# A code-book feed-forward loop with the bias as contracted rows, GELUs over two PSUM banks, and the far gates on GpSimd

## The chip, the cores and the metric

The kernel runs as one program on one core of a Trainium2 chip. It computes a whole tower of four layers. The metric is the device time of one execution in microseconds (us); the number quoted is the median of three runs. The core's engines have instruction streams of their own: TensorE (PE in the rows, PEld for its weight loads), VectorE (DVE), ScalarE (ACT), GpSimd (POOL) and SyncE (SP), which here starts transfers. They meet only at semaphores: an instruction waits until a counter has reached a value, and adds to a counter when it is done.

## The reference

The change lies in one stage, the feed-forward part of layer 2, which looks up small networks in code books. For each of 2048 tokens and each of S = 8 sub-spaces, with D = 192, R = 16, M = 64 codes, K = 4 chosen, H = 32 hidden units and G = 64:

```python
z = jnp.einsum('nd,sdr->nsr', xf, P)
scores = jnp.einsum('nsr,smr->nsm', z, C)
topv, topi = jax.lax.top_k(scores, K)
w = jax.nn.softmax(topv, axis=-1)
W1g = W1[sidx, topi]; b1g = b1[sidx, topi]
W2g = W2[sidx, topi]; b2g = b2[sidx, topi]
h = jax.nn.gelu(jnp.einsum('nsr,nskrh->nskh', z, W1g) + b1g)
yl = jnp.einsum('nskh,nskhr->nskr', h, W2g) + b2g
comb = jnp.einsum('nskr,nsk->nsr', yl, w).reshape(N, S * R)
out = jax.nn.gelu(comb @ G1 + g1b) @ G2 + g2b
```

Here xf is the layer-normalised residual, and out is added to the residual. Each code m of sub-space s has its own small network with W1[s, m] (16 by 32), b1, W2 (32 by 16) and b2; a token uses the four codes with the best scores, weighted by w.

## The kernel before

The kernel does not gather. It evaluates all 64 codes of every sub-space for every token and multiplies the hidden values by a gate, which is w for a chosen code and zero for the others. `codes_stage` (L1549) does it in `NG = 4` groups of `GT = 512` tokens. A group takes `STEPS = 32` steps: 16 for sub-spaces 0 to 3, then 16 for sub-spaces 4 to 7 (a half each). A step handles `QS = 4` units, one for each of the four sub-spaces, and a unit holds four codes of 32 hidden units, thus 128 rows by 512 tokens.

In a step, for unit j:

- TensorE forms the up product (L1740), one PSUM bank `up` each, four banks. The weights are `w1r` and the tokens `zr`, both bf16 with 96 contracted rows: a float is split into three bf16 parts, and six products of parts stand below one another in the rows.
- ScalarE applies GELU with the bias b1 as a column (L1879) and writes into `hp`, one of `HOLD = 3` step buffers in SBUF.
- VectorE multiplies by the gate (L2021). The near gates (j = 0, 1) are spread to 128 rows by a product of TensorE into the PSUM tile `gate` (L1747). The far gates (j = 2, 3) come with a DMA of 512 KB a step, issued by SyncE, from a scratch in DRAM into `wide_gates`, a ring of `GRING = 5` step slots (`bring_gates`).
- TensorE adds the down products of the step (L1767, float32: two rows of the trace for each of the four) to the accumulator `comb`. In the program's order they stand after the units of the next step, one step behind.

At a half's end ScalarE copies `comb` to `comb_t` (`keep_comb`, L1871), and TensorE starts the next half with bias products for b2 (L1758, L1762). The tail of a group (`first_last` L1724, ScalarE's GELU, `second_last` L1731, VectorE's `add_out` L2027 to the residual) runs in steps 2 to 4 of the next group.

The preparation of the next group is interleaved with the steps, as the loops over k write it out: projection (L1676), scores (L1682), the eight best of each row and the marking of four (L1967, L1981), exponentials (L1857, between two activation-table loads), the spreading of z to 96 rows (L1690), the gates' normalisation, splitting and transposition (L1698, L1708). All of TensorE's pieces go through one PSUM bank, `misc`, that ScalarE empties (`keep`, L1830). The last group prepares nothing. Ahead of the loop the same steps run for group 0, and w1 is split on VectorE and spread to `w1r` by TensorE.

The order on each engine is the order in which the program is written; no scheduler moves anything. The semaphores that matter are `up_ready`, `h_ready` (a GELU is done), `gate_ready`, `gated` (a multiplication is done), `downed` (the down products of a step), `comb_kept`, and `gates_in` (a transfer landed).

Of the kernel before, what the change touches and what calls it, by code (L numbers as in the profile page):

```python
# [1497 lines left out]
KR = SR * len(PAIRS)  # L1498
QS = SS // 2
# [4 lines left out]
BANKS = 4  # L1504
GBANKS = 2
HOLD = 3
# [3 lines left out]
GRING = 5  # L1510
# [49 lines left out]
def codes_stage(nc, m, a):  # L1560
    with Stage(nc, "cod") as s:
# [3 lines left out]
        sel_w = s.sb("sel_w", [P, 4, NPART, KR], BF16)  # L1565
        sel_g = s.sb("sel_g", [P, NBLK, P], BF16)
        b1 = s.sb("b1", [P, SS * HT])
# [6 lines left out]
        w1r = s.sb("w1r", [KR, SS, SM * SH], BF16)  # L1574
        zr = [s.sb(f"zr{i}", [KR, SS, GT], BF16) for i in range(2)]
# [3 lines left out]
        hp = [s.sb(f"hp{i}", [P, QS, GT]) for i in range(HOLD)]  # L1579
        ex = s.sb("ex", [P, GS * SS, SM])  # L1580
# [18 lines left out]
        first_bank = up + gate + [misc]  # L1599
        names = ("w_in p_in w1_in w1_split first_ready first_kept zeroed misc_ready misc_kept z_high z_low z_rest_ready z_mid "  # L1600
                 "shifted exped weighted w_high w_rest w_mid w_low up_ready gate_ready h_ready gated downed "
                 "comb_kept b2_ready dve act_own").split()
        (w_in, p_in, w1_in, w1_split, first_ready, first_kept, zeroed, misc_ready, misc_kept, z_high, z_low, z_rest_ready, z_mid,
         shifted, exped, weighted, w_high, w_rest, w_mid, w_low, up_ready, gate_ready, h_ready, gated, downed,
         comb_kept, b2_ready, dve, act_own) = (s.sem(n) for n in names)
        gates_out = s.sem("gates_out")
        gates_in = [s.sem(f"gates_in{i}") for i in range(GRING)]
        N_IN = 10
# [13 lines left out]
        def _(sp):  # L1622
# [3 lines left out]
            for dst, src in ((sel_w[:].bitcast(I16), "sel_w"), (sel_z[:].bitcast(I16), "sel_z"),  # L1626
                             (sel_g[:].bitcast(I16), "sel_g"), (b2, "S_b2"), (b2d[:], "S_b2d"), (b1[:], "S_b1"), (w2[:], "S_w2"),
                             (g1[:], "S_g1"), (g1b[:], "S_g1b"), (g2[:], "S_g2")):
                sp.dma_start(dst, a[src]).then_inc(w_in, 16)

# [28 lines left out]
        def _(pool):  # L1659
            nc.gpsimd.memset(wp[:], 0.0).then_inc(zeroed, 1)  # L1660
            pool.wait_ge(zeroed, 1)
            nc.gpsimd.memset(last_h[SG:SG + 1, :], 1.0).then_inc(zeroed, 1)

        @block.tensor
        def _(pe):
# [69 lines left out]
            def unit(g, k, j):  # L1735
                u = g * UNITS + k * QS + j
                sub, f = QS * (k // HT) + j, code_of(k, j)
                if u >= BANKS:
                    pe.wait_ge(h_ready, u - BANKS + 1)
                nc.tensor.matmul(up[u % BANKS][:], w1r[:, sub, f * P:(f + 1) * P], zr[g % 2][:, sub, :],  # L1740
                                 start=True, stop=True).then_inc(up_ready, 1)
                if j >= QP:
                    return
                if u >= QS:
                    pe.wait_ge(gated, u - QS + 1)
# [1837 lines left out]
```

## Time and profile before

| what | value |
|---|---|
| median of three runs | 3345.11 us (3338.17 to 3347.05) |
| profiled execution | 3335.59 us |
| its span | 3333.8 us |
| mean granted TensorE clock | 0.85 of full speed |
| TensorE busy | 2390.9 us (72%) |
| VectorE busy | 2309.3 us (69%) |
| ScalarE busy | 1595.2 us (48%) |
| GpSimd busy | 940.1 us (28%) |
| code-book loop, 2158 to 2621 us | 463 us |

Busy times are sums over the whole tower, whose stages have different limits, so they say little on the stage in question. The last line is a stretch of the timeline; its four groups take 124, 126, 125 and 88 us. In the tables a clock of 1.00 stands for 2.4 GHz, 0.50 for 1.2 GHz.

### The profile page before, as it was taken

What the parts mean: (1) busy time and instruction counts of PE and PEld (TensorE: products, weight loads), DVE (VectorE), ACT (ScalarE), POOL (GpSimd) and SP (SyncE); (2) the same over time, 40 slices, a digit from 0 to 9 for tenths busy, and PEclk for the clock granted to TensorE, in tenths of its full rate; (3) what the DMA queues carried; (4) which work ended last, traced back from release to release, by engine and by line L of the source; (5) the groups of instructions that cost most, each with busy time, mean ns of one, the idle gap of its engine ahead of it and who ended that gap; (6) DMA issues with size and microseconds to landing.
All of it is one profiled execution on the core that took longest, in us unless ns stands there. A gap on an engine that the chain in (4) does not pass through costs nothing. (4 is left out here: it accounts for less than half of the span.)

```text
span 3333.8 us, 38681 instructions
## 1 busy us (share of the span) xinstructions
PE 2390.9 (72%) x12580; PEld 1437.0 (43%) x12620; DVE 2309.3 (69%) x5830; ACT 1595.2 (48%) x2954; POOL 940.1 (28%) x466
## 2 busy tenths in 40 slices
PE   5869985889898877699931112688889788774457
PEld 4646652334343334499721111323222366663335
DVE  5753333999999996211278998588888699998521
ACT  3221114667665642111116773677878546654211
POOL 2000003777676761367300000000000033344032
PEclk9969996899999987799965555799999899997578
DMA  1230001111111100511100000234435400000221
GB/s 54 38 115 1 1 15 69 51 51 51 51 51 51 51 0 0 177 39 41 56 12 1 1 0 2 101 122 151 152 114 189 144 1 1 1 1 1 120 85 56
DMA packets 81796, 185.27 MB, mean 56 GB/s; under 512 B 35197, under 2 KB 52827, under 8 KB 76251
## 3 DMA queue, kind: packets, MB, share of 16 engines
q1 hardware_dynamic: 75452, 170.56, 15.3%
q0 software_dynamic: 6144, 12.25, 1.2%
q8 instruction: 101, 1.65, 0.2%
q14 instruction: 99, 0.81, 0.1%
HBM read 165.91 MB, written 24.77 MB: 57 GB/s over the span
## 5 line engine op out<-in xcount | busy, mean ns | idle before, releaser
L2243 POOL TENSOR_TENSOR mam_st<-mam_du,mam_b_rows 128x1536 f32<-128x1536 f32 x128 | 439.6, 3441 | 172.9 <-PE mam_ysum L2312 172.4
L2473 DVE TENSOR_TENSOR_SCAN mam_st<-mam_da,mam_st 128x512 f32<-128x512 f32 x384 | 441.1, 1204 | 35.9 <-ACT mam_da L2413 18.2
L2312 PE MATMUL mam_ysum<-mam_st,held_ident 128*128 128x512 f32 x768 | 389.7, 648 | 2.2 <-DVE mam_st L2479 2.2
L1879 ACT ACTIVATE cod_hp<-cod_up,cod_b 128x512 f32<-128x512 f32 x512 | 317.0, 704 | 84.3 <-PE cod_up L1740 84.3
L2413 ACT ACTIVATE mam_da<-mam_delta,mamw_decay 128x508 f32<-128x508 f32 x384 | 254.2, 683 | 185.9 <-DVE mam_st L2473 151.0
L2595 POOL TENSOR_TENSOR att_probs<-att_se,att_neg 128x1536 f32<-128x1536 f32 x16 | 55.0, 3441 | 811.8 <-DVE att_neg L2805 811.8
L2479 DVE TENSOR_TENSOR mam_st<-mam_st,mam_c_ps 128x1536 f32<-128x1536 f32 x128 | 224.4, 1753 | 17.0 <-PE mam_c_ps L2307 13.5
L2312 PEld LDWEIGHTS mam_ysum<-mam_st,held_ident 128*128 128x128 f32 x768 | 159.4, 208 | 167.5 <-issue 160.3
L692 DVE SCALAR_TENSOR_TENSOR held_h<-x_dn,held_gate,held_h 128x192 f32<-128x192 f32 x256 | 89.1, 410 | 182.5 <-PE x_dn L659 180.8
L2805 DVE MATCH_REPLACE8 att_neg<-att_top,att_neg 128x128 f32<-128x128 f32 x768 | 201.2, 275 | 0.3
L2021 DVE TENSOR_TENSOR cod_hp<-cod_hp,cod_gate 128x512 f32<-128x512 f32 x256 | 163.3, 678 | 47.4 <-ACT cod_hp L1879 46.9
L1740 PE MATMUL cod_up<-cod_zr,cod_w1r 96*128 96x512 bf16 x512 | 181.0, 392 | 15.2 <-ACT cod_hp L1879 9.4
L2021 DVE TENSOR_TENSOR cod_hp<-cod_hp,cod_wide_gates 128x512 f32<-128x512 f32 x256 | 164.6, 683 | 25.0 <-ACT cod_hp L1879 24.9
L2798 DVE MAX8 att_top<-att_neg 128x8 f32<-128x128 f32 x768 | 154.7, 278 | 21.3 <-ACT att_neg L2721 14.2
L1767 PE MATMUL cod_comb<-cod_hp,cod_w 128*16 128x512 f32 x1024 | 140.1, 620 | 26.3 <-DVE cod_hp L2021 25.6
L682 ACT ACTIVATE x_ht<-x_up 128x512 f32<-128x512 f32 x96 | 52.1, 595 | 211.5 <-PE x_up L649 211.5
L456 POOL TENSOR_TENSOR held_h<-held_h,n_y 128x768 f32<-128x768 f32 x4 | 7.4, 1846 | 484.2 <-DVE n_y L492 484.0
L659 PEld LDWEIGHTS x_dn<-x1w_w,x_ht 128*128 128x128 f32 x768 | 123.5, 190 | 35.6 <-issue 35.6
L925 ACT ACTIVATE gr_ht<-gr_up 128x512 f32<-128x512 f32 x80 | 39.2, 491 | 205.9 <-PE gr_up L863 205.9
L659 PE MATMUL x_dn<-x1w_w,x_ht 128*128 128x192 f32 x768 | 137.4, 332 | 0.0
L993 DVE TENSOR_TENSOR gr_o<-gr_dn,gr_w2c 128x192 f32<-128x192 f32 x40 | 14.3, 358 | 173.0 <-PE gr_dn L874 173.0
L2307 PE MATMUL mam_c_ps<-mam_c_part,mamw_pick 96*128 96x512 bf16 x128 | 52.2, 408 | 106.8 <-DVE mam_st L2479 101.9
(551 smaller groups left out, 5338.1 us busy)
## 6 DMA issues: line engine op xcount, KB each, us to landing
cod_wide_gates<-gate_scratch SPq DMA_DIRECT2D x128, 512.0 KB, 3.9
mam_b_rows<-b_scratch SPq DMA_DIRECT2D x32, 1024.0 KB, 7.3
slot_scratch<-in_slot_fresh SPq DMA_DIRECT2D x2, 3860.0 KB, 14.5
sw_w<-in_L_w SPq DMA_DIRECT2D x1, 6144.0 KB, 18.5
gr_w<-in_L_w SPq DMA_DIRECT2D x1, 5376.0 KB, 41.7
gr_w<-in_L_w SPq DMA_DIRECT2D x1, 4608.0 KB
sw_w<-in_L_w SPq DMA_DIRECT2D x1, 4608.0 KB, 31.0
gr_rows<-slot_scratch SPq DMA_DIRECT2D x40, 96.5 KB, 2.0
```

The costliest lines, as they stand in the source:

```text
L659: last = nc.tensor.matmul(dn[x % 2][:, t, 0:D], ht[(g * NT + f) % NHT][:, t * P:(t + 1) * P], w2_sb[:, f, :], start=(f == first[e]), stop= ...
L1740: nc.tensor.matmul(up[u % BANKS][:], w1r[:, sub, f * P:(f + 1) * P], zr[g % 2][:, sub, :], start=True, stop=True).then_inc(up_ready, 1)
L1767: last = nc.tensor.matmul(comb[32 * j:32 * j + SR, :], w2[:, sub * HT + code_of(k, j), :], hp[step % HOLD][:, j, :], start=False, stop=(k ...
L1879: nc.scalar.activation(hp[step % HOLD][:, j, :], up[u % BANKS][:], ACT.Gelu_apprx_tanh, bias=b1[:, sub * HT + f:sub * HT + f + 1]).then_in ...
L2021: nc.vector.tensor_tensor(at, at, by, ALU.mult).then_inc(gated, 1)
L2243: nc.gpsimd.tensor_tensor(st[it % N_ST][:], du[r % 2][:], along(b_rows[:, p % RING, n % PIECE, :], 1, [P, MC, MT]), ALU.mult)\
L2312: last = nc.tensor.matmul(ysum[:, c, :], m.ident[:], st[it % N_ST][:, c, :], start=False, stop=(it % DS == DS - 1))
L2413: nc.scalar.activation(live(da[:, c, :], r % 2), live(delta[r % 2][:, c, :], r % 2), ACT.Exp, scale=decay[:, c, n:n + 1]).then_inc(exp_rea ...
L2473: nc.vector.tensor_tensor_scan(fs, fa, fs, 0.0, ALU.mult, ALU.add).then_inc(scanned, 1)
L2479: nc.vector.tensor_tensor(x[:], x[:], along(c_ps[:], 1, [P, MC, MT]), ALU.mult).then_inc(weighted, 1)
L2798: last = nc.vector.max(top[:, n, :], cut[:, n, :])
L2805: last = nc.vector.match_replace(rev, top[:, n, :], rev, -BIG)
```

## The change

Six things change in the stage.

1. The bias b1 becomes three more contracted rows (99 in place of 96): the rows 96 to 98 of `w1r` hold b1's three bf16 parts, those of `zr` hold ones. VectorE splits b1 at the stage's start; SyncE carries the parts through a new scratch in DRAM into `w1r`. GpSimd sets the ones.
2. `up` becomes two tiles of two banks. `pair(g, k, h)` forms two units, and one GELU of 128 x 1024 without a bias takes both.
3. `gate` becomes one tile of two banks, and VectorE multiplies both near units in one operation.
4. Both far units are multiplied on GpSimd, in one operation of 128 x 1024, announced on a new counter `pool_gated`; down products and SyncE's transfers wait for it as well.
5. There are four step buffers, and the down products of step s - 2 (`LAG = 2`) are issued in step s, after the first pair, ahead of the gates and of the second pair. The transfer ring for far gates has four slots.
6. The preparation, the tail and the copy of `comb` move with it, the first two by two steps, the copy by one.

The diff, cut to its core (line numbers are left out; the shifts of the preparation on ScalarE and VectorE are like the one shown on TensorE):

```diff
@@ sizes @@
+KB = KR + NPART
-BANKS = 4
-GBANKS = 2
-HOLD = 3
+HOLD = 4
+LAG = 2
-GRING = 5
+GRING = 4
+N_GATED = 1
@@ tiles @@
-        w1r = s.sb("w1r", [KR, SS, SM * SH], BF16)
-        zr = [s.sb(f"zr{i}", [KR, SS, GT], BF16) for i in range(2)]
+        w1r = s.sb("w1r", [KB, SS, SM * SH], BF16)
+        zr = [s.sb(f"zr{i}", [KB, SS, GT], BF16) for i in range(2)]
-        up = [s.psum(f"up{i}", [P, 512]) for i in range(BANKS)]
-        gate = [s.psum(f"gate{i}", [P, 512]) for i in range(GBANKS)]
+        up = [s.psum(f"up{i}", [P, 2, 512]) for i in range(2)]
+        gate = s.psum("gate", [P, QP, 512])
@@ SyncE @@
+            sp.dma_start(b1[:], a["S_b1"]).then_inc(b1_in, 16)
...
+            sp.wait_ge(b1_split, NPART)
+            for p in range(NPART):
+                sp.dma_start(m.b1_scratch[p], b1_part[p][:]).then_inc(b1_out, 16)
+            sp.wait_ge(b1_out, 16 * NPART)
+            sp.dma_start(w1r[KR:KB].rearrange("o s c -> o (s c)"),
+                         m.b1_scratch.rearrange("n r p -> n (r p)")).then_inc(b1_rows, 16)
...
-                    sp.wait_ge(gated, QS * (step - GRING + 1))
+                    sp.wait_ge(gated, N_GATED * (step - GRING + 1))
+                    sp.wait_ge(pool_gated, step - GRING + 1)
@@ GpSimd @@
+            for i in range(2):
+                nc.gpsimd.memset(zr[i][KR:KB, :, :], 1.0).then_inc(ones_set, 1)
+
+            for step in range(NG * STEPS):
+                pool.wait_ge(h_ready, 2 * step + 2)
+                pool.wait_ge(gates_in[step % GRING], 16 * (step // GRING + 1))
+                at = hp[step % HOLD][:, QP:, :]
+                nc.gpsimd.tensor_tensor(at, at, wide_gates[:, step % GRING], ALU.mult).then_inc(pool_gated, 1)
@@ TensorE @@
+            def pair(g, k, h):
+                step = g * STEPS + k
+                if step:
+                    pe.wait_ge(h_ready, 2 * step + h - 1)
+                for i in range(2):
+                    j = 2 * h + i
+                    sub, f = QS * (k // HT) + j, code_of(k, j)
+                    last = nc.tensor.matmul(up[h][:, i, :], w1r[:, sub, f * P:(f + 1) * P], zr[g % 2][:, sub, :],
+                                            start=True, stop=True)
+                last.then_inc(up_ready, 1)
+
+            def gates(g, k):
+                step = g * STEPS + k
+                if step:
+                    pe.wait_ge(gated, N_GATED * (step - 1) + 1)
+                for j in range(QP):
+                    ...
+                last.then_inc(gate_ready, 1)
@@ down @@
-                pe.wait_ge(gated, QS * (step + 1))
+                pe.wait_ge(gated, N_GATED * (step + 1))
+                pe.wait_ge(pool_gated, step + 1)
@@ TensorE's loop; the pieces of the preparation and of the tail two steps later @@
-                        if k == 2:
+                        if k == 4:
                             first_last(g - 1)
...
-                    for j in range(QS):
-                        unit(g, k, j)
-                    if g + k:
-                        down(g * STEPS + k - 1)
+                    pair(g, k, 0)
+                    if g * STEPS + k >= LAG:
+                        down(g * STEPS + k - LAG)
+                    gates(g, k)
+                    pair(g, k, 1)
@@ ScalarE @@
+            def pair(g, k, h):
+                step = g * STEPS + k
+                act.wait_ge(up_ready, 2 * step + h + 1)
                 if step >= HOLD:
                     act.wait_ge(downed, step - HOLD + 1)
-                nc.scalar.activation(hp[step % HOLD][:, j, :], up[u % BANKS][:], ACT.Gelu_apprx_tanh,
-                                     bias=b1[:, sub * HT + f:sub * HT + f + 1]).then_inc(h_ready, 1)
+                nc.scalar.activation(hp[step % HOLD][:, 2 * h:2 * h + 2, :], up[h][:], ACT.Gelu_apprx_tanh)\
+                    .then_inc(h_ready, 1)
...
-                    if g + k > 1 and k % HT == 1:
+                    if g + k > LAG and k % HT == LAG:
                         keep_comb((g * STEPS + k) // HT - 1)
@@ VectorE @@
+            def near_gates(g, k):
+                step = g * STEPS + k
+                v.wait_ge(h_ready, 2 * step + 1)
+                v.wait_ge(gate_ready, step + 1)
+                at = hp[step % HOLD][:, 0:QP, :]
+                nc.vector.tensor_tensor(at, at, gate[:], ALU.mult).then_inc(gated, 1)
...
+            v.wait_ge(b1_in, 16)
+            nc.vector.tensor_copy(b1_part[0][:], b1[:]).then_inc(b1_split, 1)
+            ...
             v.wait_ge(w1_in, 16)
...
-                    for j in range(2):
-                        unit(g, k, j)
+                    near_gates(g, k)
```

On TensorE, near the end of the last group before the change (`cod_comb` products are down products, `cod_up` up products, `cod_gate` the spread near gates):

```order
L1767 MATMUL cod_comb<-cod_hp,cod_w 16x512 x4
L1740 MATMUL cod_up<-cod_zr,cod_w1r 128x512
L1747 MATMUL cod_gate<-cod_wt,cod_sel_g 128x512
L1740 MATMUL cod_up<-cod_zr,cod_w1r 128x512
L1747 MATMUL cod_gate<-cod_wt,cod_sel_g 128x512
L1740 MATMUL cod_up<-cod_zr,cod_w1r 128x512 x2
L1767 MATMUL cod_comb<-cod_hp,cod_w 16x512 x4
```

The same place after it, at the very end of the loop:

```order
L1764 MATMUL cod_up<-cod_zr,cod_w1r 128x512 x4
L1797 MATMUL cod_comb<-cod_hp,cod_w 16x512 x4
L1775 MATMUL cod_gate<-cod_wt,cod_sel_g 128x512 x2
L1764 MATMUL cod_up<-cod_zr,cod_w1r 128x512 x2
L1797 MATMUL cod_comb<-cod_hp,cod_w 16x512 x8
```

The down products moved from behind all four up products of a step to between the first pair and the gates, and are now those of the step two back; a row of four up products is the second pair of one step and the first pair of the next. At the end two steps of down products are left over.

On ScalarE, around the exponentials in the first group before the change (`cod_zr` and `cod_comb_t` are copies out of PSUM, `cod_hp` the GELUs):

```order
L1879 ACTIVATE cod_hp<-cod_up,cod_b 128x512 x4
L1830 ACTIVATE cod_zr<-cod_misc 96x512
L1857 ACT_TABLE_LOAD
L1857 ACTIVATE cod_ex<-cod_ex 128x2048
L1879 ACT_TABLE_LOAD
L1879 ACTIVATE cod_hp<-cod_up,cod_b 128x512 x4
L1830 ACTIVATE cod_zr<-cod_misc 96x512
L1879 ACTIVATE cod_hp<-cod_up,cod_b 128x512 x4
L1871 ACTIVATE cod_comb_t<-cod_comb 128x512
```

And after it:

```order
L1912 ACTIVATE cod_hp<-cod_up 128x1024 x2
L1864 ACTIVATE cod_zr<-cod_misc 96x512
L1891 ACT_TABLE_LOAD
L1891 ACTIVATE cod_ex<-cod_ex 128x2048
L1912 ACT_TABLE_LOAD
L1912 ACTIVATE cod_hp<-cod_up 128x1024 x2
L1905 ACTIVATE cod_comb_t<-cod_comb 128x512
L1864 ACTIVATE cod_zr<-cod_misc 96x512
```

The exponentials kept their distance from the other pieces, while the copy of `comb` at the half boundary came one step nearer to them: two GELUs stand between, where eight did.

## Rows read from the trace of the kernel before

**Rows 1.** Windows of the four groups: start:end, length, busy of PE, PEld, DVE, ACT, POOL, PEclk.
```profile
2158.00:2282.00 124.00, 106.82 (x555) 33.11 (x566) 103.63 (x258) 99.57 (x166) 0.00 (x0) 0.93 0.46 154
2282.00:2408.00 126.00, 107.89 (x576) 34.46 (x588) 105.91 (x262) 99.44 (x166) 0.00 (x0) 0.96 0.42 141
2408.00:2533.00 125.00, 108.86 (x573) 34.47 (x580) 105.12 (x261) 98.58 (x164) 0.00 (x0) 0.95 0.43 139
2533.00:2621.00 88.00, 83.95 (x486) 23.01 (x486) 78.11 (x130) 77.22 (x130) 0.00 (x0) 1.00 0.51 170
```

**Rows 2.** TensorE's timeline, two steps without preparation: start, duration, operation.
```profile
2402.91 1.05 PE L1767 MATMUL cod_comb<-cod_hp,cod_w 128*16 128x512 f32 x8
...
2403.89 0.39 PE L1740 MATMUL cod_up<-cod_zr,cod_w1r 96*128 96x512 bf16 x1
...
2405.31 1.05 PE L1767 MATMUL cod_comb<-cod_hp,cod_w 128*16 128x512 f32 x8
```

**Rows 3.** Groups of instructions by shape, whole run: busy, mean ns, idle before.
```profile
L2243 POOL TENSOR_TENSOR mam_st<-mam_du,mam_b_rows 128x1536 f32<-128x1536 f32 x128 | 439.6, 3441 | 172.9 <-PE mam_ysum L2312 172.4
...
L1879 ACT ACTIVATE cod_hp<-cod_up,cod_b 128x512 f32<-128x512 f32 x512 | 317.0, 704 | 84.3 <-PE cod_up L1740 84.3
...
L2021 DVE TENSOR_TENSOR cod_hp<-cod_hp,cod_gate 128x512 f32<-128x512 f32 x256 | 163.3, 678 | 47.4 <-ACT cod_hp L1879 46.9
...
L1767 PE MATMUL cod_comb<-cod_hp,cod_w 128*16 128x512 f32 x1024 | 140.1, 620 | 26.3 <-DVE cod_hp L2021 25.6
...
L682 ACT ACTIVATE x_ht<-x_up 128x512 f32<-128x512 f32 x96 | 52.1, 595 | 211.5 <-PE x_up L649 211.5
...
L456 POOL TENSOR_TENSOR held_h<-held_h,n_y 128x768 f32<-128x768 f32 x4 | 7.4, 1846 | 484.2 <-DVE n_y L492 484.0 <-ACT n_y L538 0.2
...
L1849 ACT ACTIVATE cod_z_part<-held_xw 128x1024 bf16<-128x1024 f32 x4 | 4.2, 1057 | 0.0
```

**Rows 4.** ScalarE's and TensorE's timelines at a half boundary.
```profile
2410.28 0.60 ACT L1871 ACTIVATE cod_comb_t<-cod_comb 128x512 f32<-128x512 f32 x1
...
2410.93 1.47 PE L1758 MATMUL cod_comb<-cod_wt,cod_b_part 128*32 128x512 bf16 x12 [0.76 <-ACT cod_comb_t L1871]
...
2413.31 1.05 PE L1767 MATMUL cod_comb<-cod_hp,cod_w 128*16 128x512 f32 x8
```

**Rows 5.** TensorE's timeline, pieces of the preparation.
```profile
2304.71 1.98 PE L1676 MATMUL cod_misc<-held_xt,cod_proj 96*128 96x512 f32 x4
...
2306.53 0.38 PE L1740 MATMUL cod_up<-cod_zr,cod_w1r 96*128 96x512 bf16 x1
...
2308.91 1.13 PE L1682 MATMUL cod_misc<-cod_codes,held_xw 128*128 128x256 f32 x4
...
2338.51 0.85 PE L1690 MATMUL cod_misc<-cod_z_part,cod_sel_z 128*96 128x512 bf16 x3
```

**Rows 6.** TensorE's timeline, the second product of a group's tail.
```profile
2422.24 0.92 PE L1731 MATMUL cod_misc<-cod_g,cod_last_h 65*128 65x192 f32 x4 [0.49 <-DVE held_h L2027]
```

**Rows 7.** ScalarE's timeline around the exponentials.
```profile
2343.84 0.59 ACT L1830 ACTIVATE cod_zr<-cod_misc 96x512 bf16<-96x512 f32 x1
...
2348.96 2.42 ACT L1879 ACTIVATE cod_hp<-cod_up,cod_b 128x512 f32<-128x512 f32 x4
```

**Rows 8.** TensorE's timeline, down products after a wait.
```profile
2328.60 1.91 PE L1767 MATMUL cod_comb<-cod_hp,cod_w 128*16 128x512 f32 x8 [1.39 <-DVE cod_hp L2021]
...
2334.45 1.06 PE L1767 MATMUL cod_comb<-cod_hp,cod_w 128*16 128x512 f32 x8
```

**Rows 9.** TensorE's timeline, the stage's first down product.
```profile
2167.74 1.05 PE L1767 MATMUL cod_comb<-cod_hp,cod_w 128*16 128x512 f32 x8
```

**Rows 10.** DMA issues: KB each, median us from issue to landing.
```profile
cod_wide_gates<-gate_scratch SPq DMA_DIRECT2D x128, 512.0 KB, 3.9
```

**Rows 11.** GpSimd's and VectorE's timelines in the Mamba stage.
```profile
602.02 3.43 POOL L2243 TENSOR_TENSOR mam_st<-mam_du,mam_b_rows 128x1536 f32<-128x1536 f32 x1 [2.82 <-PE mam_ysum L2312]
...
601.90 3.45 DVE L2473 TENSOR_TENSOR_SCAN mam_st<-mam_da,mam_st 128x512 f32<-128x512 f32 x3 [0.68 <-ACT mam_da L2413]
```

More of the change, by code:

```diff
@@ L1579, in codes_stage @@
         hp = [s.sb(f"hp{i}", [P, QS, GT]) for i in range(HOLD)]
+        at_first = hp[NPART][:].rearrange("p j t -> p (j t)")
+        sel_cols = 4 * NPART * KR // 2
+        sel_w = at_first[:, 0:sel_cols].bitcast(BF16).rearrange("p (q n r) -> p q n r", q=4, n=NPART)
+        b1 = at_first[0:SS * HT, sel_cols:sel_cols + P]
+        b1_part = [at_first[0:SS * HT, sel_cols + P + i * P // 2:sel_cols + P + (i + 1) * P // 2].bitcast(BF16)
+                   for i in range(NPART)]
         ex = s.sb("ex", [P, GS * SS, SM])
@@ L1733, in second_last @@
                 last.then_inc(misc_ready, 1)
[L1735 to L1745, printed above, removed]
-                half, code = f // NBLK, f % NBLK
-                nc.tensor.matmul(gate[j][:], sel_g[:, code, :], wt[g % 2][:, 2 * (QP * (k // HT) + j) + half, :],
-                                 start=True, stop=True).then_inc(gate_ready, 1)
+            def pair(g, k, h):
[13 more added lines that the diff above has]
+                for j in range(QP):
+                    f = code_of(k, j)
+                    half, code = f // NBLK, f % NBLK
+                    last = nc.tensor.matmul(gate[:, j, :], sel_g[:, code, :],
+                                            wt[g % 2][:, 2 * (QP * (k // HT) + j) + half, :], start=True, stop=True)
+                last.then_inc(gate_ready, 1)
             def down(step):
@@ L1812, in _ @@
[L1812 to L1818 removed]
+                        if 7 <= k < 9:
+                            misc_turn(turn + Z_AT + k - 7)
+                            project(g + 1, k - 7, misc, misc_ready)
@@ new lines, in _ @@
+                        if 9 <= k < 13:
+                            misc_turn(turn + SC_AT + k - 9)
+                            score(g + 1, k - 9, misc, misc_ready)
+                        if 14 <= k < 22:
+                            misc_turn(turn + ZR_AT + k - 14)
+                            spread_z(g + 1, k - 14, misc, misc_ready)
+                        if 25 <= k < 27:
+                            misc_turn(turn + GF_AT + k - 25)
+                            turn_gates(g + 1, k - 25, misc, misc_ready)
@@ L1819, in _ @@
+                        if 27 <= k < 31:
+                            misc_turn(turn + WT_AT + k - 27)
+                            turn_w(g + 1, k - 27, misc, misc_ready)
+                    pair(g, k, 0)
[3 more added lines that the diff above has]
+                    pair(g, k, 1)
                 if g + 1 < NG:
                     pe.wait_ge(misc_kept, prep_turn(g + 1) + N_PREP)
-            down(NG * STEPS - 1)
+            for i in range(LAG):
+                down(NG * STEPS - LAG + i)
@@ L2080, in _ @@
[L2080 to L2092 removed]
+                        if 10 <= k < 14:
+                            v.wait_ge(misc_kept, prep_turn(g + 1) + SC_AT + k - 10 + 1)
+                            bests(k - 10)
@@ new lines, in _ @@
+                        if 15 <= k < 19:
+                            mark_best(k - 15, 0)
+                        if 19 <= k < 23:
+                            weights(g + 1, k - 19)
+                        if 20 <= k < 24:
+                            normed(k - 20)
+                        if 24 <= k < 28:
+                            low_w(g + 1, k - 24)
+                    if g + 1 < NG:
+                        if k == 11:
+                            low_z(g + 1)
+                        if 11 <= k < 15:
+                            shift(g + 1, k - 11)
+                        if 15 <= k < 19:
+                            mark_best(k - 15, 1)
+                        if 19 <= k < 23:
+                            totals(k - 19)
+                        if 22 <= k < 26:
+                            rest_w(g + 1, k - 22)
```

133 lines of the change are left out of this document (42 added, 91 removed).

## The prediction

> **What bounds the kernel now.** I read the granted clock and the 40 slices first, to find the stage; then busy times in four windows, one for each group of 512 tokens; then TensorE's timeline inside a group; then the durations of the operations; then what ended each wait.
>
> The code loop takes 463 us of the span of 3333.8, about 14%; nothing else in the kernel changes [rows 1]. The last group, which prepares no successor, takes 88 us, and there TensorE is busy 84 and granted the full 2.4 GHz; the two middle groups take 126 and 125 [rows 1]. So there are two limits. In a step without preparation TensorE sets the pace: down products start at 2402.91 and again at 2405.31, a step of 2.40 us; it splits into 0.98 (2402.91 to 2403.89) for the four down products and 1.42 for six bf16 products, 0.22 each and a switch of 0.1 [rows 2]. In a step with preparation VectorE does: 27.8 us more in a middle group than in the last (105.91 less 78.11) come on top of four multiplications a step of 678 ns [rows 1, 3], and 25.6 of TensorE's idle time in the loop stands before the down products, released by the multiplication [rows 3]. The step is a chain, up product, GELU, multiplication, down product, one step deep, so each late multiplication stops TensorE.
>
> **The change part by part.** The hand-over from one engine to the next costs 0.05 us (ScalarE's copy ends at 2410.28 + 0.60 = 2410.88, TensorE starts at 2410.93) [rows 4].
>
> VectorE loses the two far multiplications, and its two near ones become one operation of 1024 columns, at most 2 x 678 = 1.36 us [rows 3]: 43.5 a group, and with 27.8 of preparation 71 of some 119. It is then no bound, and its waits before the down products go.
>
> ScalarE: four GELUs of 704 ns become two over two banks without bias. The GELU without bias takes 595 at 512 columns, so 1.19 for two; a copy over 1024 takes 1057 [rows 3]. I take 1.06, between 0.70 and 1.19, since the copy has the same width. That is 67.8 a group, against 77 in the last one now [rows 1].
>
> GpSimd has no operation in the loop now [rows 1], and gets 128 multiplications of 1024 columns from two tiles in SBUF. Its multiplications take 3441 at 1536 columns and its additions 1846 at 768 [rows 3]: a slope of 2.077 ns a column, so 1846 + 256 x 2.077 = 2378 ns, 2.38 us, bounded by 1.85 and 3.44. By itself that fits under the step, but it is in the chain.
>
> The chain now: counted from the start of down(s-2), the down products end at 0.98; the two gates at 1.42; the first of pair 1 starts there, the second at 1.64 and lasts 0.39; GELU 1 starts at 2.08 and ends at 3.14; GpSimd runs from 3.19 to 5.57; down(s) may start at 5.62. These are two steps, so 2.81 a step, above TensorE's own 2.40. The cause is the place of the down products ahead of pair 1: its up products wait behind the products two steps back, which wait for GpSimd. With 1.85 or 3.44 for GpSimd a step is 2.54 or 3.34. A fourth step buffer doesn't loosen it, for it is TensorE's order that closes the loop. VectorE's near gates start at 1.47 and end by 2.83, so 2.8 us of preparation may come between before they delay anything.
>
> Steps with preparation are set by TensorE once the sum of 2.40 and the piece exceeds 2.81. The projection costs 1.82 (2304.71 to 2306.53), with a switch 1.92; a score 1.13 less the overlap of 0.16 seen there, with a switch 1.07; a spread 0.85 less 0.16, 0.68 [rows 5]. The tail's first product I set like a projection, the second at 0.9 from its 0.92 [rows 6]; the transposes at 0.8, an estimate from the spread.
>
> A middle group, step by step. Step 2: the comb tile must be copied before the next bias products. GELU 1 of the step before starts 2.08 after down, then comes GELU 0, then the copy, which ends at about 4.6; the bias products take 2.38 (2410.93 to 2413.31) [rows 4]: 7.0. Steps 4 to 12: 9 x 2.40 = 21.6, pieces 1.92 + 2 x 0.9 + 2 x 1.92 + 4 x 1.07 = 11.8, and 3.8 of waits: twice 1.5, since the next product needs the addition to the residual, which now stands behind a multiplication whose gates come late in the step (0.05 + 1.36 + 0.5 for three quarters of 678 ns, less 0.44 for pair 1), and 0.8, since the first score's copy stands behind a GELU and the rounding of z: 37.2. Seven spread steps at 3.08: 21.6. Step 18: ScalarE's two table loads and exponentials keep it from GELU for 5.1 us (2343.84 to 2348.96) [rows 7]; then come GELU 1, GELU 0 and the comb copy, which ends at 8.7, and 2.38: 11.1. After such a wait TensorE ran at 1.2 GHz once: down to down took 5.85 (2328.60 to 2334.45), against 2.40 + 0.68 for such a step, so 2.8 lost [rows 8]; I take 1.7, between 0 and 2.8: 12.8. Six steps with transposes: 6 x 3.2 = 19.2. The other eight, two of them behind a stall at 2.40: 21.7. Sum 119.5, against 125.5 now.
>
> The first group: 10.7 to its first down product, 2167.74 now and one step later afterwards, though a shorter one: 2168.7 [rows 9]; then 119.5 less 7.0 (step 2), 6.7 (the tail's 3.7 and its two waits of 1.5), 5.4 (steps 0 and 1), plus 1.9 for what is left of step 2: 102.3. Together 113, now 124. The last group: two boundaries 14.0, three tail steps 7.2 + 3.7 + 1.5 = 12.4, 26 steps at 2.76 (2.81 but for the three behind a stall) 71.8, the last step 0.4 and its drain 5.62 + 1.05 = 6.7: 105, now 88. So the last group loses 17 and the first three win 23.
>
> Sum: 113 + 119.5 + 119.5 + 105 = 457 against 463: -6. The setup gains four VectorE operations on 128 columns and two more trips through DRAM. These lie beside TensorE's products that spread w1, but the small operations stand ahead of the splitting of w1: +1.3, between 0 and 2.7 (a transfer of 512 KB lands in 3.9 [rows 10], a small one sooner, if w1's own doesn't hide it). In all -5. The ones rows cost nothing: GpSimd sets them while the weights are being spread. Ring of 4 for the far gates: SP may issue a transfer once GpSimd has finished the step four earlier, three steps or 8.4 us ahead of use, and it lands in 3.9 [rows 10]; behind SP's wait stand only later transfers. The down product's added wait holds up the gates and pair 1, which is the loop above. 99 rows in place of 96 I take to cost TensorE nothing: the gates' products have 128, and all six together take 1.42 [rows 2].
>
> **From the trace to the time.** The profiled execution took 3335.6, its span 3333.8. The median of the runs is 3345.1, so the profiled one is 9.5 below it. 3335.6 - 5 = 3331, and for the median 3345.1 - 5 = 3340.
>
> **The rivals.** First, that the chain does not bind: if GpSimd needs 1.56 or less (5.62 - 2 x 0.41 = 4.80, two steps of 2.40), or TensorE issues pair 1 earlier than I think, then the last group returns to about 91, and in the other groups eight steps win 0.4 each: 14 + 3 x 3.3, less what the boundaries keep, some -18 more: 3322. For it speaks that spans on GpSimd are rough; against it that 768 and 1536 columns give 2.40 and 2.24 ns a column, nowhere near 1.5. Chance 0.15.
>
> Second, the clock, on the slower side. Each of the seven half boundaries now keeps TensorE idle for about 2.2 us in one piece (the copy behind two GELUs). Before, 0.76 there left it at full speed [rows 4], while two waits of 1.39 close together brought 1.2 GHz [rows 8]. If each boundary loses the 2.8 us of that spell: 7 x 2.8 = 20, and 3360. It decides from the point where an idle piece of 2.2 us is enough by itself. Chance 0.2.
>
> Third, GpSimd and VectorE hinder each other. In the Mamba stage VectorE's scans, with two inputs in SBUF, start at 601.90 and run three in 3.45 while GpSimd's multiplication runs from 602.02 for 3.43, and neither is stretched [rows 11]: so here the trace shows no exclusion. Were there one, up to 27.8 of preparation a group [rows 1] would hold GpSimd up, and GpSimd's 2.38 VectorE in turn; about half of the preparation has two tile inputs, so between 14 and 28 a group, I take 20: 3340 + 60 = 3400. Chance 0.08.
>
> The Trainium skill, "SBUF — State Buffer", section "SBUF: two separate sides", says that a VectorE operation with two SBUF inputs and a GpSimd operation that reads SBUF share a port pair, held for a whole instruction, so that one blocks the other. By that rule the third rival would be the forecast; [rows 11] disagree with it, and so it gets little.
>
> That the change does not do what it says is covered by none of these; for that and mishaps elsewhere (code loading, transfers) 0.05.
>
> **How the numbers follow.** The forecast's case has 0.52, with a range of its own from 3329 (GpSimd at 2.2, no slow spell) to 3352 (GpSimd at 2.6, 2.8 at every step 18). About 0.3%, 10 us, is what a measurement of this kernel can tell from no change. Faster than 3335: a third of the forecast's case and nearly all of the first rival, with 0.02 of the rest: 0.34. Slower than 3355: most of the second, the third, and 0.03: 0.28. Within: 0.38. The range takes in the first rival with a margin for GpSimd at 1.85, and the second with some of GpSimd at 2.6 and more: 3314 to 3366; the third lies outside.
>
> **What would show it.** A plain step of 2.81 in the last group, which then takes 105, TensorE waiting before the comb product for GpSimd; GpSimd's multiplication at 2.38; GELU at 1.06 and VectorE no longer the one that releases the down products; about 119 in the middle groups; a wait of some 5 us at step 18. Wrong it would be if the last group stays near 90 (no loop), if the granted clock falls at the half boundaries (second rival), or if GpSimd's operation is longer in the groups with preparation than in the last (third).

## The result and the profile after

The changed kernel takes 3381.64 us (median of four, 3377.31 to 3386.27) against 3341.64 for the kernel before in its four runs: a ratio of 1.0123, 95% interval 1.0104 to 1.0142. It is slower by 40 us, where 5 us less was forecast, and lies above the range.

The stage accounts for it. From the first projection to the first down product it took 70.3 us before (2097.47 to 2167.74) and 73.9 after (2106.94 to 2180.82); from the first down product to the last, 452.4 before and 491.0 after: 3.6 + 38.6 = 42. The profiled execution is 51 longer than that of before because it already stands 9.5 later when the stage begins, in code that did not change; in most of the runs below the stage begins at 2094 to 2100 again, so this is the spread of single executions.

The four groups of the changed kernel, for [rows 1], with the same columns:

```profile
2170.00:2300.00 130.00, 109.08 (x564) 33.67 (x565) 76.78 (x162) 86.93 (x101) 76.79 (x32) 0.88 0.44 142
2300.00:2434.00 134.00, 112.07 (x586) 35.12 (x584) 78.34 (x165) 85.65 (x101) 78.66 (x33) 0.91 0.41 131
2434.00:2568.00 134.00, 111.52 (x587) 34.75 (x588) 77.97 (x165) 86.54 (x102) 78.24 (x33) 0.91 0.41 132
2568.00:2674.00 106.00, 88.00 (x493) 23.54 (x486) 38.79 (x33) 62.60 (x67) 75.47 (x32) 0.97 0.42 144
```

The last group takes 106, as forecast (105). The groups with preparation take 130 and 134, where 113 and 119.5 were forecast: the whole error is there. VectorE's busy time fell by only 27 in a middle group (105.1 to 78.0), though it lost more work than that: its multiplications fell from 78.1 to 38.8 in the last group. The other 12 are operations that became longer. The groups of instructions in the loop, for [rows 3], show which:

```profile
L2047 DVE TENSOR_TENSOR cod_hp<-cod_hp,cod_gate 128x1024 f32<-128x1024 f32 x128 | 155.7, 1217 | 229.9 <-PE cod_gate L1775 204.5 <-ACT cod_hp L1912 25.2 <-issue 0.2
L2031 DVE TENSOR_TENSOR cod_ex<-cod_ex,cod_total 128x512 f32<-128x512 f32 x12 | 19.1, 1593 | 0.0
...
L2019 DVE SCALAR_TENSOR_TENSOR cod_ex<-held_xw,cod_ex 128x512 f32<-128x512 f32 x12 | 18.7, 1556 | 0.0
L2005 DVE TENSOR_TENSOR cod_ex<-held_xw,held_logits 128x512 f32<-128x512 f32 x12 | 18.1, 1506 | 0.3
...
L1994 DVE TENSOR_TENSOR cod_z_part<-cod_ex,cod_z_part 128x1024 bf16<-128x1024 f32 x3 | 9.4, 3118 | 0.0
L2025 DVE TENSOR_REDUCE cod_total<-cod_ex 128x8 f32<-128x512 f32 x12 | 8.1, 676 | 0.1
```

In the kernel before, the operations of L2031, L2019 and L2005 took 684, 685 and 685 ns and that of L1994 1215. All four have two inputs in SBUF. Their rows there, under the line numbers of the kernel before:

```profile
L1974 DVE TENSOR_TENSOR cod_ex<-held_xw,held_logits 128x512 f32<-128x512 f32 x12 | 8.2, 685 | 0.3
L1988 DVE SCALAR_TENSOR_TENSOR cod_ex<-held_xw,cod_ex 128x512 f32<-128x512 f32 x12 | 8.2, 685 | 0.0
L2000 DVE TENSOR_TENSOR cod_ex<-cod_ex,cod_total 128x512 f32<-128x512 f32 x12 | 8.2, 684 | 0.0
L1963 DVE TENSOR_TENSOR cod_z_part<-cod_ex,cod_z_part 128x1024 bf16<-128x1024 f32 x3 | 3.6, 1215 | 0.0
```

The reduction (one input, 677 before) and the near gates (one input in PSUM, 1217 against 1214 in far_on_vector below, where GpSimd is idle) kept their length. GpSimd's multiplication, in the same list, whose waits are for ScalarE:

```profile
L1684 POOL TENSOR_TENSOR cod_hp<-cod_hp,cod_wide_gates 128x1024 f32<-128x1024 f32 x128 | 309.2, 2415 | 247.8 <-ACT cod_hp L1912 247.2
```

VectorE's wait stands in busy time and not in idle time, so no releaser names it. One step shows how it works, the fourteenth of a middle group, VectorE first:

```profile
2348.67 3.12 DVE L1994 TENSOR_TENSOR cod_z_part<-cod_ex,cod_z_part 128x1024 bf16<-128x1024 f32 x1
2351.89 2.64 DVE L2005 TENSOR_TENSOR cod_ex<-held_xw,held_logits 128x512 f32<-128x512 f32 x1
...
2354.49 1.18 DVE L2047 TENSOR_TENSOR cod_hp<-cod_hp,cod_gate 128x1024 f32<-128x1024 f32 x1
```

GpSimd in the same stretch:

```profile
2348.34 2.36 POOL L1684 TENSOR_TENSOR cod_hp<-cod_hp,cod_wide_gates 128x1024 f32<-128x1024 f32 x1 [0.52 <-ACT cod_hp L1912]
2351.20 2.78 POOL L1684 TENSOR_TENSOR cod_hp<-cod_hp,cod_wide_gates 128x1024 f32<-128x1024 f32 x1 [0.50 <-ACT cod_hp L1912]
```

and TensorE:

```profile
2350.85 1.05 PE L1797 MATMUL cod_comb<-cod_hp,cod_w 128*16 128x512 f32 x8 [0.35 <-POOL cod_hp L1684]
2355.73 1.03 PE L1775 MATMUL cod_gate<-cod_wt,cod_sel_g 128*128 128x512 bf16 x2 [3.83 <-DVE cod_hp L2047]
```

VectorE's 3.12 ends 1.1 after GpSimd's 2.36 has ended at 2350.70, its 2.64 ends 0.55 after 2353.98: each did all but about 0.13 of its own 1.22 and 0.69 us of work after GpSimd was done. GpSimd's second multiplication, begun while VectorE's first operation still ran, is 0.4 longer, as it had to wait in turn. Who starts first is not held up: an operation with two inputs in SBUF that began before GpSimd's kept its 1.22, and GpSimd's, begun 0.9 before its end, took 3.12 in place of 2.36:

```profile
2344.37 1.22 DVE L1990 TENSOR_TENSOR cod_ex<-held_xw,cod_z_part 128x1024 f32<-128x1024 f32 x1
...
2344.69 3.12 POOL L1684 TENSOR_TENSOR cod_hp<-cod_hp,cod_wide_gates 128x1024 f32<-128x1024 f32 x1 [1.36 <-ACT cod_hp L1912]
```

So these two engines do not meet only at semaphores, as was said of all of them at the start: here each waits for the other with no semaphore between them. In step 14 the near gates stand behind both operations, and TensorE waits 3.83 us to overwrite the gate tile: 8.8 us for a step that should take 3.1.

### The profile page after: what moved, and what is told of

Same layout as the page of the kernel before. It is cut to its first block and busy times, and to the rows that moved or that the text cites. A ratio compares the mean times of both kernels' runs of the same rounds, so it can differ in the third digit from the quotient of the medians.

```text
span 3384.4 us, 37961 instructions
## 1 busy us (share of the span) xinstructions
PE 2404.2 (71%) x12620; PEld 1438.5 (43%) x12620; DVE 2191.1 (65%) x5450; ACT 1540.7 (46%) x2698; POOL 1257.2 (37%) x596
## 5 line engine op out<-in xcount | busy, mean ns | idle before, releaser
L2503 DVE TENSOR_TENSOR_SCAN mam_st<-mam_da,mam_st 128x512 f32<-128x512 f32 x384 | 441.1, 1204 | 35.9 <-ACT mam_da L2443 18.2
L1684 POOL TENSOR_TENSOR cod_hp<-cod_hp,cod_wide_gates 128x1024 f32<-128x1024 f32 x128 | 309.2, 2415 | 247.8 <-ACT cod_hp L1912 247.2
L2342 PE MATMUL mam_ysum<-mam_st,held_ident 128*128 128x512 f32 x768 | 397.4, 659 | 2.2 <-DVE mam_st L2509 2.2
L1912 ACT ACTIVATE cod_hp<-cod_up 128x1024 f32<-128x1024 f32 x256 | 254.5, 1021 | 149.8 <-PE cod_up L1764 147.3
L2047 DVE TENSOR_TENSOR cod_hp<-cod_hp,cod_gate 128x1024 f32<-128x1024 f32 x128 | 155.7, 1217 | 229.9 <-PE cod_gate L1775 204.5
L2509 DVE TENSOR_TENSOR mam_st<-mam_st,mam_c_ps 128x1536 f32<-128x1536 f32 x128 | 224.4, 1753 | 16.2 <-PE mam_c_ps L2337 12.8
L1764 PE MATMUL cod_up<-cod_zr,cod_w1r 99*128 99x512 bf16 x512 | 151.2, 396 | 2.9 <-ACT cod_hp L1912 1.6
```

What stands on the lines that cost most here:

```text
L1684: nc.gpsimd.tensor_tensor(at, at, wide_gates[:, step % GRING], ALU.mult).then_inc(pool_gated, 1)
L1764: last = nc.tensor.matmul(up[h][:, i, :], w1r[:, sub, f * P:(f + 1) * P], zr[g % 2][:, sub, :], start=True, stop=True)
L1912: nc.scalar.activation(hp[step % HOLD][:, 2 * h:2 * h + 2, :], up[h][:], ACT.Gelu_apprx_tanh)\
L2047: nc.vector.tensor_tensor(at, at, gate[:], ALU.mult).then_inc(gated, 1)
L2342: last = nc.tensor.matmul(ysum[:, c, :], m.ident[:], st[it % N_ST][:, c, :], start=False, stop=(it % DS == DS - 1))
L2503: nc.vector.tensor_tensor_scan(fs, fa, fs, 0.0, ALU.mult, ALU.add).then_inc(scanned, 1)
```

## The experiments

The table gives the time between a group's first down product and the next group's (the last group: to its last one), read from the down products' rows of each run, and the ratio to the kernel before in the runs that were taken together with each (their medians lie between 3337 and 3342).

| kernel | g0 | g1 | g2 | g3 | median us | ratio (95%) |
|---|---|---|---|---|---|---|
| before | 120.1 | 125.4 | 125.1 | 81.7 | 3341.6 | |
| changed | 129.0 | 133.2 | 133.1 | 95.8 | 3381.6 | 1.0123 (1.0104 to 1.0142) |
| one_input | 113.7 | 120.2 | 119.8 | 94.2 | 3340.5 | 1.0012 (0.9996 to 1.0028) |
| pair1_first | 120.2 | 126.2 | 126.2 | 82.5 | 3347.3 | 1.0039 (1.0022 to 1.0055) |
| copy_back | 120.9 | 126.5 | 124.9 | 92.1 | 3354.5 | 1.0058 (1.0037 to 1.0079) |
| far_on_vector | 121.9 | 126.1 | 126.2 | 83.1 | 3348.9 | 1.0038 (1.0018 to 1.0058) |
| all_vector | 120.1 | 125.6 | 124.3 | 81.7 | 3341.3 | 1.0014 (1.0001 to 1.0026) |
| all_gpsimd | 122.4 | 126.4 | 126.3 | 82.5 | 3347.8 | 1.0033 (1.0023 to 1.0043) |
| far_copy | 111.7 | 118.3 | 120.9 | 81.0 | 3327.0 | 0.9961 (0.9947 to 0.9974) |
| far_copy_add | 112.9 | 115.0 | 116.4 | 79.4 | 3312.6 | 0.9918 (0.9905 to 0.9932) |
| gpsimd_copy_add | 120.6 | 122.6 | 122.8 | 90.6 | 3341.3 | 1.0007 (0.9981 to 1.0032) |

**The two-input operations taken away.** Each of the seven preparation operations, for groups 1 to 3, becomes a reduction, as here:

```diff
+                if g:
+                    nc.vector.tensor_reduce(lone[:, t, 16:24], ex[:, cols, :], AX.X, ALU.add).then_inc(weighted, 1)
+                    return
                 nc.vector.tensor_tensor(ex[:, cols, :], ex[:, cols, :], along(total[:, cols], 2, full),
                                         ALU.mult).then_inc(weighted, 1)
```

> Seven preparation operations of VectorE in the loop (for groups 1 to 3), those with two inputs in SBUF, are replaced by reductions that read one of the two inputs, so they take as long but their results are missing (the gates of groups 1 to 3 are not the reference's). Theory A, exclusion: VectorE's two-input operations and GpSimd's multiplication wait for each other whole. Then those seven go back from 1.5 to 3.1 us to 0.4 to 1.2 us, the step with the first spread from 8.8 to about 3.1, the steps with the gates' sums from 4.3, 5.7 and 6.6 to about 2.8 each, a middle group from 133 to about 119, the last group stays at 95.8, and the time falls by about 40 us, to 3340. Theory B, VectorE's work is simply late behind the near gates: the replaced operations are as long as the unstretched ones, the waits stay, a middle group stays within 130 to 133 and the time within 10 us of 3381.

Theory A to the number: a middle group 120, the time 3340.5. The reductions do not stretch, and GpSimd is down to its own length:

```profile
L1685 POOL TENSOR_TENSOR cod_hp<-cod_hp,cod_wide_gates 128x1024 f32<-128x1024 f32 x128 | 302.4, 2363 | 211.3 <-ACT cod_hp L1913 210.8
...
L2045 DVE TENSOR_REDUCE cod_lone<-cod_ex 128x8 f32<-128x512 f32 x12 | 8.1, 678 | 0.0
```

VectorE had as many operations as in the changed kernel, each about as long as the original when nothing meets it, so late work was not the cause; their two SBUF inputs were. That a reduction also writes less does not explain it: the near gates write 1024 columns and kept 1.22 us beside GpSimd. Not all of the 13 is the operations themselves: the half boundary between two groups fell from 8.5 to 6.9, as its bias products ran at 2.4 GHz, while steps 6 and 7 became longer by about as much.

**The second pair first.**

```diff
                     pair(g, k, 0)
-                    if g * STEPS + k >= LAG:
-                        down(g * STEPS + k - LAG)
                     gates(g, k)
                     pair(g, k, 1)
+                    if g * STEPS + k >= LAG:
+                        down(g * STEPS + k - LAG)
```

> On TensorE the gates and the second pair are issued ahead of the down products of the step two back; nothing else changes. Theory A, the chain through GpSimd closes only because the second pair stands behind the down products: a plain step of the last group falls from 2.84 to about 2.42 (GpSimd's 2.37 and a hand-over), the last group from 95.8 to about 84, and the middle groups by 5 or less, as their waits are others: 3381 less 12 less 15 at most, 3355 to 3369. Theory B, the pace is GpSimd's latency wherever the products stand: the plain step stays at 2.84 and the time at 3381.

The chain closes where theory A put it: the plain step of the last group is 2.39 and 2.54 in turn, 2.47 on average, and the group falls by 13. TensorE's rows of two such steps:

```profile
2597.43 1.05 PE L1797 MATMUL cod_comb<-cod_hp,cod_w 128*16 128x512 f32 x8
...
2599.82 1.05 PE L1797 MATMUL cod_comb<-cod_hp,cod_w 128*16 128x512 f32 x8
...
2602.36 1.05 PE L1797 MATMUL cod_comb<-cod_hp,cod_w 128*16 128x512 f32 x8
```

In the changed kernel these go in pairs of 5.66 (2652.46 to 2658.12), with GpSimd as the releaser of every second one:

```profile
2652.46 1.05 PE L1797 MATMUL cod_comb<-cod_hp,cod_w 128*16 128x512 f32 x8 [0.82 <-POOL cod_hp L1684]
...
2654.85 1.05 PE L1797 MATMUL cod_comb<-cod_hp,cod_w 128*16 128x512 f32 x8
...
2658.12 1.05 PE L1797 MATMUL cod_comb<-cod_hp,cod_w 128*16 128x512 f32 x8 [0.82 <-POOL cod_hp L1684]
```

It also took 7 from the middle groups, more than the 5 expected (2.9 of them at the half boundary, which fell from 8.5 to 5.6), so that 3347.3 lies below the expected 3355.

**The copy back by a step.**

```diff
-                    if g + k > LAG and k % HT == LAG:
+                    if g + k > LAG - 1 and k % HT == LAG - 1:
                         keep_comb((g * STEPS + k) // HT - 1)
```

> ScalarE's copy of the comb tile goes back by one step, between the two GELUs of step 1 (or 17) of a half, where it stood before the change; the rest is as in the changed kernel. Theory A, at a half boundary TensorE pays an idle piece of 2 us or more and, because of it, a spell at 1.2 GHz: the idle piece goes, the bias products go back from 3.8 to 2.4 us, the boundary falls from 8.4 to about 5.2, and that of step 18 from 12.5 to about 8.5: 25 us in all, 3356. Theory B, the bias products are slow for another reason: they stay at 3.8, and only the idle pieces go: about 15 us, 3366.

As theory A said: 3354.5, a boundary of 4.77 (5.2 expected). Step 18 fell further than expected, from 12.5 to 5.8, but the step after it rose from 3.0 to 4.6. The boundary in the last group of the changed kernel, TensorE:

```profile
2621.28 1.05 PE L1797 MATMUL cod_comb<-cod_hp,cod_w 128*16 128x512 f32 x8
...
2625.83 2.01 PE L1787 MATMUL cod_comb<-cod_wt,cod_b_part 128*32 128x512 bf16 x12 [2.09 <-ACT cod_comb_t L1905]
...
2629.61 1.23 PE L1797 MATMUL cod_comb<-cod_hp,cod_w 128*16 128x512 f32 x8
```

and with the copy back:

```profile
2585.72 1.05 PE L1797 MATMUL cod_comb<-cod_hp,cod_w 128*16 128x512 f32 x8
...
2588.11 1.47 PE L1787 MATMUL cod_comb<-cod_wt,cod_b_part 128*32 128x512 bf16 x12
...
2590.49 1.05 PE L1797 MATMUL cod_comb<-cod_hp,cod_w 128*16 128x512 f32 x8
```

The idle 2.09 is gone, and the bias products with it go from 3.78 to 2.38, the time that they take at 2.4 GHz (granted clock 0.61 from 2625.8 to 2629.6 in the changed kernel, 1.00 from 2588.1 to 2590.4 here). But the idle piece alone does not decide: in one_input the same 2.09 stands at the same place and the bias products take 2.38, at a granted clock of 1.00:

```profile
2577.78 1.47 PE L1788 MATMUL cod_comb<-cod_wt,cod_b_part 128*32 128x512 bf16 x12 [2.09 <-ACT cod_comb_t L1906]
2580.16 1.05 PE L1798 MATMUL cod_comb<-cod_hp,cod_w 128*16 128x512 f32 x8
```

What else brings the clock down there stays open.

**The far gates on VectorE.** GpSimd's loop goes, and between the two blocks of preparation of each step VectorE does:

```diff
+            def far_gates(g, k):
+                ...
+                nc.vector.tensor_tensor(at, at, wide_gates[:, step % GRING], ALU.mult).then_inc(pool_gated, 1)
```

> Both far gates are multiplied by VectorE in one operation of 1024 columns in place of GpSimd; all else stays as in the changed kernel, TensorE's order too. Theory A, exclusion and the chain through GpSimd's 2.4 us are what was lost: the plain step falls from 2.84 to 2.40, the last group from 95.8 to about 85, the seven two-input operations take their 0.4 to 1.2 us again, a middle group falls from 133 to about 118: some 55 us in all, 3325. Theory B, the two-step lag with its later gates and its half boundaries is what costs: a middle group stays above 125 and VectorE, with two operations of 1.2 a step and the preparation, is the bound again: 3350 or more.

The last group falls as expected, to 83, and the operations are back at 0.68 us. But a middle group falls to 126 and not to 118: with 2.4 us of multiplications a step VectorE itself is late in steps 14 and 22 to 25 (around step 14 it is busy for all of the 10.0 us from 2336 to 2346). Theory A had left this out; for the middle groups and the time theory B was nearer (above 125, and 3350 or more).

**A probe of forms** (one execution, read for its trace). In the last group, after a short reduction, one extra operation a step:

```diff
+                if 3 <= k < 7:
+                    own.step(nc.vector.tensor_tensor(c, a, b, ALU.mult))
+                elif 7 <= k < 11:
+                    own.step(nc.vector.tensor_tensor_scan(c, a, b, 0.0, ALU.mult, ALU.add))
+                ...
```

> As the changed kernel, but in the last group, which prepares nothing, VectorE runs one extra operation of 512 columns a step on spare data, a little after GpSimd's multiplication has begun: a multiplication of two float32 tiles in SBUF (steps 3 to 6), a scan over two such tiles (7 to 10), a float32 copy (11 to 14), a multiplication of two bf16 tiles (19 to 22), a reduction of one tile (23 to 26). Theory A, what is locked out is a multiplication or subtraction with two inputs in SBUF, but not a scan, which reads two inputs at half the pace: the multiplications take about 0.7 us and wait up to 2, thus 2 to 2.7 in the trace, the scan its 1.2, the reduction 0.7; on the copy the theory has no row and leaves 0.4 or above 2 open. Theory B, the Mamba stage's scans were not locked out because of something in that stage: the scan is stretched here too, above 2 us. Theory C, an operation is stretched by GpSimd's traffic and not locked out: all forms are longer by the same share.

```profile
2600.57 2.57 DVE L2100 TENSOR_TENSOR cod_ex<-cod_ex 128x512 f32<-128x512 f32 x1
...
2605.16 1.29 DVE L2102 TENSOR_TENSOR_SCAN cod_ex<-cod_ex 128x512 f32<-128x512 f32 x1
...
2608.00 2.54 DVE L2102 TENSOR_TENSOR_SCAN cod_ex<-cod_ex 128x512 f32<-128x512 f32 x1
...
2627.64 2.06 DVE L2104 COPY cod_ex<-cod_ex 128x512 f32<-128x512 f32 x1
...
2660.11 0.69 DVE L2108 TENSOR_REDUCE cod_total<-cod_ex 128x1 f32<-128x512 f32 x1
```

GpSimd beside the two scans:

```profile
2602.99 2.38 POOL L1684 TENSOR_TENSOR cod_hp<-cod_hp,cod_wide_gates 128x1024 f32<-128x1024 f32 x1 [0.40 <-ACT cod_hp L1912]
2607.10 2.36 POOL L1684 TENSOR_TENSOR cod_hp<-cod_hp,cod_wide_gates 128x1024 f32<-128x1024 f32 x1 [1.73 <-ACT cod_hp L1912]
```

Theory B holds, A fails on the scan: one that GpSimd leaves alone but for 0.2 us takes 1.29, one that meets its multiplication 2.54, ending 1.08 after GpSimd's end at 2609.46. The float32 copy waits as well: its four lengths run from 0.89 to 2.13, but each of the four ends 0.28 after a multiplication of GpSimd (the one shown after that from 2627.07 to 2629.42). So do the four bf16 multiplications (1.30 to 2.29), while the float32 ones end 0.54 or 0.55 after and the scans 1.08 or 1.09: how long an operation becomes depends on when it starts, and what is left when GpSimd is done depends on its form. The reduction never waits (0.69 in all four, beside GpSimd), so theory C falls.

**The edits together.** all_vector is far_on_vector, pair1_first and copy_back in one, with b1 split behind w1; all_gpsimd is the same without far_on_vector.

> The changed kernel with four edits together: both far gates on VectorE in one operation, the gates and the second pair ahead of the down products, the comb copy between the two GELUs of step 1, and the splitting of b1 behind that of w1. If the savings add up: from the run with the far gates on VectorE (3348.9), four boundaries 6.9 to 4.8, three steps at the exponentials 16.7 to 10.4, some 1 us for each of three tails, 2 for the setup: 3317, faster than the kernel before by 0.6%. If VectorE is the bound behind these waits, they come back in the steps after: 3335, no different from the kernel before.

> The same with the far gates left on GpSimd: second pair ahead of the down products, the comb copy between the two GELUs, b1 split behind w1. If the savings add up: from the run with the second pair first (3347.3), four boundaries 5.6 to 4.8, three steps at the exponentials 15.3 to 10.4, 2 for the setup: 3327. The exclusion stays: the two-input operations keep 1.5 us and more, and the steps 23 to 25 their 5 us each, so this one is slower than that with the far gates on VectorE by about 10. If the exclusion no longer matters once the waits are shifted, both are equal.

Neither sum came out (all_vector is nearer to its second number, and all_gpsimd is slower than it by 6.5 where about 10 was expected): boundaries stay at 5.6 and the steps at the exponentials at 12 and more. With the second pair first, the down products stand at the end of the step, and the copy between the two GELUs waits for them, so the second GELU does too: the two edits undo each other.

**Without the second pair first.** far_copy is far_on_vector and copy_back with b1 split behind w1; far_copy_add also has, on VectorE:

```diff
-                    near_gates(g, k)
                     if g:
                         if 5 <= k < 7:
                             add_out(g - 1, k - 5)
+                    near_gates(g, k)
```

> The changed kernel with three edits: far gates on VectorE in one operation, the comb copy between the two GELUs of step 1 or 17, b1 split behind w1; TensorE's order as changed, with the down products ahead of the gates and the second pair. (With the second pair first, the copy had to wait for down products at the end of the same step, and brought nothing.) If the savings of the two single runs add up: four boundaries 6.9 to 4.8, three pairs of steps at the exponentials 16.6 to 10.4, against the run with the far gates on VectorE; the loop goes from 457.4 to about 430, the setup saves 2: 3349 - 29 = 3320, faster than the kernel before by 0.5%. If VectorE needed the time in which it was waiting at the exponentials, part comes back in the steps after: 3332.

> As the run far_copy, and VectorE's addition to the residual stands ahead of the multiplication by the near gates in steps 5 and 6. If the waits of the tail (4.7 and 5.8 for the two steps, of which 3.3 and 4.3 are work) come from that multiplication, 1.5 us goes in each of two steps of three groups: 9 us less than far_copy, 3311. If the wait is for another thing, both are equal.

far_copy lands between its two numbers, far_copy_add is the fastest, 0.8% under the kernel before. Its two tail steps fall from 4.7 and 5.8 to 3.1 and 4.1, so the wait was for the multiplication; the loop is 8.2 shorter than in far_copy (423.8 against 431.9), as expected (9). The median fell by 14; the other 6 are not explained, and both kernels spread over 11 to 14 us.

**The far gates' place alone.** As far_copy_add, with the far gates left on GpSimd as in the changed kernel:

> As far_copy_add, with the far gates back on GpSimd: so the changed kernel with the comb copy back by a step, the addition ahead of the near gates and b1 split behind w1. What the place of the far gates costs by itself: the last group from 79.4 to about 90.5 (the chain, 2.84 against 2.39 a step), and the middle groups from 115 to 116 to 122 to 124 (the exclusion at the steps 14 and 23 to 25): some 30 us more than far_copy_add, 3341, no different from the kernel before. If the far gates on GpSimd cost only the chain, it is 11 us more, 3324.

As expected, in the last group (90.6), the middle groups (122.6 and 122.8) and the time (3341.3). GpSimd costs 29 us in this order against VectorE, 11 of them in the last group.

## Why the prediction was wrong

- The chain through GpSimd: right. A plain step was put at 2.81 and is 2.83 (5.66 for two), GpSimd at 2.38 and 2.36 where nothing meets it, the last group at 105 and 106; pair1_first shows that the place of the down products closes it. That the last group came out so close is partly luck: its two half boundaries took 8.5 and 8.3, not 7.0 each, and the rest was shorter by as much.
- GELU over two banks at 1.06, measured 1.02; 99 rows cost nothing that shows (a plain step in far_on_vector takes 2.38 to 2.39, 2.40 before); the shorter ring held nothing up (247.2 of GpSimd's 247.8 us of idle time in the loop were ended by ScalarE). Right.
- "2.8 us of preparation may come between before they delay anything", and with it a middle group at 119.5: this step failed. It took VectorE's preparation at the length it had with GpSimd idle. A middle group was 133.2: step 14 at 8.8 instead of 3.1; steps 23 and 24 at 4.3 and 5.7 instead of 2.8, step 25 at 6.6 instead of 3.2; and step 2, two points below. one_input gives 120 back.
- The third rival had the mechanism, at 20 a group and a chance of 0.08; measured 13 to 15. It was set aside on a false reading of [rows 11]: "VectorE's scans, with two inputs in SBUF". The code allocates mam_da in PSUM, so the scans there read one SBUF input. The probe's scan, with both inputs in SBUF, waits. And the trace of before did hold the answer, beside GpSimd's additions that the prediction took its slope from [rows 3]: VectorE's product of n_y and n_gain, both in SBUF by the code, takes 0.41 at the median of 16 and 1.95 where it starts just behind such an addition:

```profile
518.86 1.81 POOL L456 TENSOR_TENSOR held_h<-held_h,n_y 128x768 f32<-128x768 f32 x1 [2.52 <-DVE n_y L492]
...
518.93 1.95 DVE L500 SCALAR_TENSOR_TENSOR held_xw<-n_y,n_rstd,n_gain 128x192 f32<-128x192 f32 x1
```

It ends 0.21 after GpSimd. The Trainium skill, "SBUF — State Buffer", section "SBUF: two separate sides", says just this: a VectorE operation in a two-port mode, or one with two SBUF inputs against a GpSimd operation that reads SBUF, and a GpSimd operation shut each other out, whole instruction against whole instruction, and whichever starts first goes first. The runs agree: the operations with two SBUF inputs wait and make GpSimd wait (3.12 for 2.36), the reduction does not; no run here shows in which mode the copy ran.
- The second rival came in part: the bias products ran at 1.2 GHz for at least part of every half boundary of the changed kernel, and step 2 took 8.5, not 7.0: 1.5 in each, where the rival had 2.8.
- Step 18 at 12.8, measured 12.5; steps 4 to 12 at 37.2, measured 35.9. Right.
- The setup at 1.3 (0 to 2.7) was 2.9 to the first up product. The split of b1, which waits for b1's transfer, stands ahead of that of w1 and took 2.04 (first row at 2113.65, w1's at 2115.69). About 1.0 of it is GpSimd again, so "the ones rows cost nothing" was wrong here: the first cast took 1.22, ending 0.09 after GpSimd had filled in the ones (at 2114.78); in one_input the same cast, begun just before the end of that fill, took 0.23, and in far_copy w1's own cast, beside the fill, took 3.67 in place of 2.29. What is left, 0.9, is open: whether w1 had landed by then no row shows.

```profile
2107.82 6.96 POOL L1678 MEMSET cod_zr<- 3x4096 bf16 x2
...
2113.65 1.22 DVE L2056 CAST cod_hp<-cod_hp 128x128 bf16<-128x128 f32 x1 [15.73 <-DMA cod_hp<-in_S_b]
...
2115.69 2.29 DVE L2063 CAST cod_hp<-cod_wide_gates 128x4096 bf16<-128x4096 f32 x1
```

## What to carry to other kernels

Before work goes to GpSimd, list what VectorE does at the same time and where each operand of it lives, by the allocation in the code and not by the name in the row; operations with both inputs in SBUF are drawn out by what is left of GpSimd's, without a wait that the trace would name. And look at each operation that stands in the program between a result and the wait for it: here the places of a copy, an addition and a split were worth 40 us with the far gates on GpSimd (3381.6 to 3341.3), more than the engine's 29.

## What was not expected of the hardware

A float32 copy of 512 columns from SBUF to SBUF, with one input, also waited for GpSimd (in all four, up to 2.13 us), while a reduction with one input did not (0.69). A cast from float32 to bf16, with one input, waited even for a GpSimd fill, which reads nothing (1.22 in place of 0.23 us). And TensorE, idle for the same 2.09 us at the same boundary, went on at 2.4 GHz in one kernel and at 1.2 GHz in another.
